# A graph network's first block: tile products ahead of the turns of the edge lists, the edge list sent later, 20 message fetches issued there

## What is computed

```python
h = jnp.maximum(_layernorm(x, axis=-1), 0.0)
hw = jnp.einsum('ni,rio->rno', h, weight)          # 8 relations and one for the node itself
msg = hw[rel, src] + bias[rel]
agg = jax.ops.segment_max(msg, dst, num_segments=n)
agg = jnp.where((in_deg > 0)[:, None], agg, 0.0)
x = x + jax.nn.relu(hw[-1] + agg + bias[-1])
```

## Time and profile before

| what | us |
|---|---|
| median of 3 runs | 2628.93 |
| lowest and highest run | 2625.03, 2635.14 |
| the profiled execution, whole | 2634.49 |
| its span in the profile | 2632.6 |

### The profile page before, as it was taken

How to read it: one execution, slowest core, us unless ns; L and a number is a source line. 1 busy time by engine, 2 the same in 40 slices (tenths; PEclk the granted TensorE clock), 3 DMA queues, 4 the chain that set the end, 5 groups by cost and what they waited for, 6 DMA issues and landing times. The chain is left out here.

```text
span 2632.6 us, 33489 instructions
## 1 busy us (share of the span) xinstructions
PE 1954.5 (74%) x11712; PEld 1074.2 (41%) x11712; DVE 1325.4 (50%) x3186; ACT 673.2 (26%) x1332; POOL 1470.4 (56%) x1528
## 2 busy tenths in 40 slices
PE   6844444545454545437899999998999999799996
PEld 2411111111111111115455555554555555467775
DVE  6466666666666666653322222321233332357775
ACT  3344454545454545433200000000000000100000
POOL 4277777777777777760256666664666666300000
PEclk8856665656556656568999999999999999899998
DMA  5545555555555555564444544565444444610000
GB/s 170 192 120 159 170 171 159 176 164 164 159 164 159 169 163 180 160 196 169 142 163 150 166 156 153 170 123 167 144 164 154 145 142 152 99 40 1 1 6 21
DMA packets 183330, 370.17 MB, mean 141 GB/s; under 512 B 38760, under 2 KB 119254, under 8 KB 174838
## 3 DMA queue, kind: packets, MB, share of 16 engines
q1 hardware_dynamic: 129208, 263.74, 28.3%
q0 software_dynamic: 48704, 101.21, 16.4%
q10 hardware_dynamic: 5246, 3.03, 0.4%
HBM read 232.54 MB, written 135.28 MB: 140 GB/s over the span
## 5 line engine op out<-in xcount | busy, mean ns | idle before, releaser
L925 POOL DMA_INDIRECT arena<-table_rel,key_rel x784 | 771.8, 984 | 277.9 <-issue 235.3
L1575 POOL DMA_INDIRECT arena<-table_cut,src_at x324 | 311.6, 962 | 275.3 <-DMA table_cut<-Z 111.9
L1040 PE MATMUL ps_t<-arena 128*128 128x50 f16 x1568 | 95.3, 212 | 471.8 <-DVE arena L953 471.8
L943 DVE SCALAR_TENSOR_TENSOR arena<-arena,keep_max 128x128 f32<-128x128 f32 x784 | 275.0, 351 | 332.4 <-DMA arena<-table_rel,key_rel 319.1
L1575 POOL DMA_INDIRECT arena<-table_next,src_at x324 | 313.3, 967 | 187.2 <-issue 91.7
L1097 ACT ACTIVATE arena<-ps_out 128x800 fp8e4<-128x800 f32 x512 | 399.8, 835 | 43.9 <-PE ps_out L1053 43.4
L1053 PE MATMUL ps_out<-arena 128*128 128x400 f16 x1024 | 370.9, 499 | 46.2 <-ACT arena L1097 46.2
L1853 PE MATMUL ps_out<-arena,Z 128*128 128x512 fp8e4 x1600 | 352.3, 380 | 0.0
L1853 PE MATMUL ps_out<-arena,cut 128*128 128x512 fp8e4 x1600 | 350.2, 379 | 0.0
L1040 PEld LDWEIGHTS ps_t<-arena 128*128 128x128 f16 x1568 | 78.2, 115 | 552.5 <-DVE arena L953 535.0
L959 DVE TENSOR_TENSOR arena<-iota,arena 128x1072 f16<-128x1072 f16 (+1 forms) x384 | 271.4, 707 | 0.0
(11 more groups left out here) (312 smaller groups left out, 1903.7 us busy)
## 6 DMA issues: line engine op xcount, KB each, us to landing
arena<-adjacency SPq DMA_DIRECT2D x64, 1600.0 KB, 7.1
adjacency<-arena SPq DMA_DIRECT2D x160, 320.0 KB
running_rows<-arena SPq DMA_DIRECT2D x392, 128.0 KB
arena<-adjacency_plain SPq DMA_DIRECT2D x50, 400.0 KB, 8.7
table_rel<-arena SPq DMA_DIRECT2D x25, 512.0 KB, 2.7
arena<-table_rel,key_rel POOLq DMA_INDIRECT x784, 2.9
adjacency_plain<-adj SPq DMA_DIRECT2D x50, 128.0 KB, 2.5
arena<-table_cut,src_at POOLq DMA_INDIRECT x324
```

The lines of the kernel that those rows point to most:

```text
L925: e.indirect_dma_start(message(t), None, table, bass.IndirectOffsetOnAxis(key[:, t:t + 1], 0)).then_inc(s_msg[t % both], 16)
L943: e.scalar_tensor_tensor(fold(t), fold(t - 1), g.keep_max[:, t:t + 1], message(t), ALU.add, ALU.max).then_inc(s_run, 1)
L1040: e.matmul(out[:, :, w * WIN:(w + 1) * WIN], g.hot_low[:, q % 2, w // 2, :, w % 2], g.hot_flat[:, q % 2, w // 2, :, w % 2].rearrange("p (a ...
L1575: e.indirect_dma_start(g.picked[:, w % 2 * BLOCKS + k, :, :].rearrange("p a f -> p (a f)"), None, tables[y], bass.IndirectOffsetOnAxis(g.s ...
```

## The change

In block 1:
- SP no longer sends the edge list ahead of all table stores, but between the stores of tiles 3 and 4 (`LISTED`).
- DVE leaves `variance` and `normal` of rounds 3 and 4 until the near destinations are counted; ACT takes `squares` of those rounds behind tiles 2 and 5 and `deviation` behind tiles 10 and 11. Tiles 0 and 1 come ahead of `squares(3)`.
- PE runs all 25 tiles and only then the 13 turns and three blocks. `turned` has two PSUM buffers (the second is where the tiles' transposes were, so that the first turn waits for the last of ACT's copies, `s_tT`); a turn waits for the reads of the last but one.
- POOL, behind its gathers of windows and blocks, waits for all table stores and issues the first 20 message fetches (`AHEAD`). What DVE keeps in the ring of messages at that time is moved into `g.Z`.

In block 2 POOL starts at fetch 20, and the wait of `step(t)` for `s_begun` counts from there.

```diff
+AHEAD, LISTED = 20, 4
-    spot0, valid = (msgf[:, 1408 + k * P:1408 + (k + 1) * P] for k in range(2))
+    spot0, valid = (g.Z[:, 8 + k, :] for k in range(2))
-    near_node, inside, code, real = (msgf[:, 1664 + k * P:1664 + k * P + RUN] for k in range(4))
+    near_node, inside, code, real = (g.Z[:, 10 + k, 0:RUN] for k in range(4))
-    turned = g.ps_t[:, 1, :].rearrange("p (f c) -> p f c", f=FIELDS)
+    turned = [g.ps_t[:, k, :].rearrange("p (f c) -> p f c", f=FIELDS) for k in range(2)]
@@ prepare, gpsimd, behind the gathers of L237
+            for k in range(2):
+                e.wait_ge(s_st[k], 16 * ((NT + 1 - k) // 2))
+            e.wait_ge(s_nst, 16)
+            for t in range(AHEAD):
+                e.indirect_dma_start(message(g, t), None, g.table8,
+                                     bass.IndirectOffsetOnAxis(g.key_rel[:, t:t + 1], 0)).then_inc(s_msg[t], 16)
@@ sync
-            e.wait_ge(s_list, 1)
-            e.dma_start(g.edge_list.rearrange(...), lists.rearrange(...)).then_inc(s_lst, 16)
             for n in range(NT):
+                if n == LISTED:
+                    e.wait_ge(s_list, 1)
+                    e.dma_start(g.edge_list.rearrange(...), lists.rearrange(...)).then_inc(s_lst, 16)
                 e.wait_ge(s_ev, n + 1)
@@ scalar
-            for r in range(2, TROUNDS):
-                squares(r)
-                deviation(r)
-                if r > 2:
-                    tile(r - 3)
-            for n in range(2, NT):
+            squares(2)
+            deviation(2)
+            for n in range(NT):
                 tile(n)
+                if n in (2, 5):
+                    squares(3 + n // 5)
+                if n in (10, 11):
+                    deviation(n - 7)
@@ vector
             normal(2)
-            variance(3)
             moments(4)
-            normal(3)
-            variance(4)
-            normal(4)
@@ behind s_ends (L437)
+            variance(3)
+            variance(4)
+            normal(3)
+            normal(4)
             e.wait_ge(s_begin, 1)
@@ tensor, turn
-                if gr:
-                    e.wait_ge(s_read, 2 * gr)
+                if gr == 0:
+                    e.wait_ge(s_tT, NT)
+                elif gr == 1:
+                    e.wait_ge(s_win, 4)
                 else:
-                    e.wait_ge(s_win, 4)
+                    e.wait_ge(s_read, 2 * gr - 2)
                 for f in range(FIELDS):
-                    last = e.transpose(turned[:, f, :], windows[gr][:, f::FIELDS], g.ident[:, :])
+                    last = e.transpose(turned[gr % 2][:, f, :], windows[gr][:, f::FIELDS], g.ident[:, :])
@@ tensor
-                if n >= NT - GROUPS + 1:
-                    turn(n - (NT - GROUPS + 1))
-            turn(GROUPS - 1)
+            for gr in range(GROUPS):
+                turn(gr)
@@ aggregate_and_build
-            for t in range(STEPS):
+            for t in range(AHEAD, STEPS):
-                e.wait_ge(s_begun, min(t + BEHIND, STEPS))
+                if t + BEHIND > AHEAD:
+                    e.wait_ge(s_begun, min(t + BEHIND, STEPS) - AHEAD)
```

More of the change, by code:

```diff
@@ L134, in edge_rows, with prepare @@
     yield tile[P - 1:P, 0:E - (P - 1) * STEPS], ap[(P - 1) * STEPS:E].rearrange("(a t) -> a t", a=1)
-def prepare(g, weight, bias):
+def prepare(g, weight, bias, s_msg):
     nc = g.nc
@@ L469, in _ @@
                 at = slice(gr * P, (gr + 1) * P)
+                fields = turned[gr % 2]
                 e.wait_ge(s_turn, gr + 1)
-                step(e.scalar_tensor_tensor(spot0, turned[:, 0, :], float(-gr * P * WIN), twice, ALU.add, ALU.subtract))
+                step(e.scalar_tensor_tensor(spot0, fields[:, 0, :], float(-gr * P * WIN), twice, ALU.add, ALU.subtract))
                 step(e.scalar_tensor_tensor(valid, spot0, -1.0, spot0, ALU.add, ALU.mult))
-                e.scalar_tensor_tensor(g.low[:, at], valid, 0.0, turned[:, 1, :], ALU.is_equal, ALU.mult).then_inc(s_read, 1)
-                e.scalar_tensor_tensor(g.both_spots[:, :, at], turned[:, 2:4, :], 2.0,
+                e.scalar_tensor_tensor(g.low[:, at], valid, 0.0, fields[:, 1, :], ALU.is_equal, ALU.mult).then_inc(s_read, 1)
+                e.scalar_tensor_tensor(g.both_spots[:, :, at], fields[:, 2:4, :], 2.0,
                                        spot0.unsqueeze(1).to_broadcast([P, 2, P]), ALU.mult, ALU.add).then_inc(s_read, 1)
@@ L479, in _ @@
                 e.wait_ge(s_turn, GROUPS + k + 1)
-                fields = [turned[:, f, 0:RUN] for f in range(FIELDS)]
+                fields = [turned[(GROUPS + k) % 2][:, f, 0:RUN] for f in range(FIELDS)]
                 step(e.scalar_tensor_tensor(near_node, fields[0], float(-(DENSE + k * (RUN // CAP // PARTS_OF)) * P), bases,
@@ L579, in _, with message @@
             e.matmul(g.ps_t[0:1, 0, 0:1], g.whole[:, :], g.ones[:, 0:1], start=True, stop=True).then_inc(s_order, 1)
+def message(g, t):
+    return g.msg[:, t % (2 * HALF) // HALF, t % HALF, :]
 class Norm:
@@ L860, in scalar, with aggregate_and_build @@
                          scale=g.inv_dev[:, n:n + 1]).then_inc(self.s_h, 1)
-def aggregate_and_build(g, table, key, params):
+def aggregate_and_build(g, table, key, params, s_msg):
     nc = g.nc
-    s_msg = [g.sem(f"msg{u}") for u in range(2 * HALF)]
     s_out = [g.sem(f"rout{h}") for h in range(2)]
@@ L889, in pairs_before @@
         return sum(b < FULL for b in order[:q]) * PAIRS
-    def message(t):
-        return g.msg[:, t % both // HALF, t % HALF, :]
     def fold(t):
@@ L924, in _ @@
                 e.sem_inc(s_begun, 1)
-                e.indirect_dma_start(message(t), None, table,
+                e.indirect_dma_start(message(g, t), None, table,
                                      bass.IndirectOffsetOnAxis(key[:, t:t + 1], 0)).then_inc(s_msg[t % both], 16)
@@ L942, in step @@
                     e.wait_ge(s_run, t)
-                e.scalar_tensor_tensor(fold(t), fold(t - 1), g.keep_max[:, t:t + 1], message(t),
+                e.scalar_tensor_tensor(fold(t), fold(t - 1), g.keep_max[:, t:t + 1], message(g, t),
                                        ALU.add, ALU.max).then_inc(s_run, 1)
@@ L2131, in gnn_kernel @@
         g.ps_out = ctx.enter_context(nc.psum_tensor("ps_out", [P, 2, 1536], F32))
-        prepare(g, a["L0_gnn_weight"].rearrange("r k o -> k r o"), a["L0_gnn_bias"].rearrange("r o -> (r o)"))
-        aggregate_and_build(g, g.table8, g.key_rel, plain_params(g, a))
+        s_msg = [g.sem(f"msg{u}") for u in range(2 * HALF)]
+        prepare(g, a["L0_gnn_weight"].rearrange("r k o -> k r o"), a["L0_gnn_bias"].rearrange("r o -> (r o)"), s_msg)
+        aggregate_and_build(g, g.table8, g.key_rel, plain_params(g, a), s_msg)
         g.recycle()
```

7 lines of the change are left out of this document (4 added, 3 removed).

## The result

| | before | after |
|---|---|---|
| median, us (20 runs each) | 2633.39 | 2619.32 |
| lowest and highest | 2625.03, 2637.59 | 2613.59, 2629.08 |
| the profiled execution: whole, span | 2634.49, 2632.6 | 2618.36, 2615.5 |

The changed kernel takes 0.995 of the time, with an interval of 0.994 to 0.9959: 14.1 us less, where 23.3 were forecast. The time forecast was 2606 us with a range of 2592 to 2619, and 2619.32 lies just above it. Both kernels ran 20 times; the 3 runs shown of before had a median 4.5 us lower than these 20.

What follows compares the result with a forecast made beforehand. Block 2 was taken to be bound by POOL's issue of 784 message fetches. Gain 29.3 less 6 us given back is 23.3; from the median 2628.9 that gives 2605.6, rounded 2606 us, range 2592 to 2619.

Steps and rivals of the forecast that it cites:

- T: Block 1: the end of the tile stage (last tile's bias), forecast at 98.4 us, 18.5 us before 116.86.
- The stall goes: Block 1, tiles 0 to 11: ACT's 13.34 us wait for the first store vanishes; tile 11 ends at 55.0, 15.1 us gained.
- The moved normalisation: Block 1, DVE: variance and normal of rounds 3 and 4 fit its idle time; cost nothing, or up to 1 us.
- Tiles 12 to 24: Block 1: tiles without turns take 2.78 us each, plus 2.5 us for gathers; stage ends at 98.4, 18.5 us gained.
- The rival of a late tile stage: Block 1: low clock or contention ends the stage near 108 to 112, 2617 us; with a larger stretch, chance 0.13.
- The turns behind: Block 1: 13 windows at 1.33 us and three blocks follow the tiles; DVE leaves at 126.5; move costs about 10 us.
- 20 fetches in block 1: Block 1, POOL: starts 4.8 us after the tile stage, fetches take 25.0 us, POOL leaves at 128.2, behind DVE.
- no charge: Block 1: fetches beside DVE's reads of windows are not stretched, citing 0.94 us at 74.58; priced at nothing.
- Block 2 starts 1.1 us later: Boundary of blocks 1 and 2: fetch 20 starts about 1.1 us after POOL's last, at 129.3 us; 29.3 us gained.
- What block 2 gives back: Start of block 2: DVE, catching up out of step, stretches about 24 fetches; 6 us lost, bounds 0 and 13.
- The last rival (the port to the end): Block 2: DVE stays out of step and stretches fetches to the end; 0.5% slower, about 2642 us; chance 0.04.

Runs made afterwards that it cites:

- experiment 4: Kernel before plus only the 20 fetches issued in block 1; old order of tiles and turns, edge list first, normalisation where it was: ratio 1.001 to before.
- experiment 8: Kernel before, with POOL's drain (its wait for the DMAs it issued) left out at the end of block 1: ratio 1.0009 to before.
- experiment 13: The changed kernel itself, run again on another chip: 2620.63 us, ratio 0.9957 to before.
- Experiment 6: Changed kernel, but the edge list is sent ahead of all table stores again (LISTED = 0): ratio 0.999 to before.
- Experiment 7: Changed kernel, but 12 turns stand between tiles 13 to 24 again, in one PSUM buffer: ratio 0.9954 to before.
- experiment 1: Changed kernel without POOL's drain (its wait for the DMAs it issued) at the end of block 1: 2612.97 us, ratio 0.9922 to before.
- experiment 2: Changed kernel with 12 fetches ahead instead of 20 (AHEAD = 12): 2625.37 us, ratio 0.9966 to before.
- experiment 5: Changed kernel, but the one-hots of block 2's first 60 folds read their indices from PSUM instead of SBUF: ratio 0.9954 to before.
- 14: Changed kernel without POOL's drain at the end of block 1, run again on another chip: 2612.47 us, ratio 0.9922 to before.
- 9: The changed kernel itself, run again on a chip where every kernel took some 2950 us: ratio 0.9969 to before.
- 15: Changed kernel without POOL's drain at the end of block 1 and with 28 fetches ahead: 2613.60 us, ratio 0.9929 to before.
- 3: Changed kernel with no fetch taken ahead (AHEAD = 0), only the new order of block 1: ratio 1.0006 to before.
- 16: Changed kernel without POOL's drain at block 1's end, turns between the tiles again, 8 fetches ahead: 2611.84 us, ratio 0.992 to before.

## Why the prediction was right and wrong

The difference, first between the two profiled executions: fetch 20 came 23.0 us earlier (158.56 and 135.56), fetch 20 to 60 took 5.4 us more (51.65 and 57.08), fetch 60 to 783 0.6 less. That makes 18.2 at fetch 783. Behind it 1.1 us went in the later layers, to which the change does nothing, and 1.0 outside the span, which gives 16.1 for the whole executions. The one of before lay 1.1 over its median of 20, the one of after 1.0 under its own: 14.1.

That pair of executions flatters the change. The old order of block 1 has two more profiles: T was 114.64 us in experiment 4 and 113.05 in experiment 8 (before without the drain), against 116.86. The new order has eight, with T from 97.0 to 103.3 and 99.8 in the mean. So T moved by some 15 us in the mean and not by 17.8 (an estimate from these eleven profiles). Fetch 783 of experiments 8 and 13, taken as second profiles of before and after, lies at 1138.2 and 1129.4; with two profiles of each the difference there is 13.5 us, close to the 14.1 of the medians.

1. *The stall goes*: right. Tile 11 ended at 55.58 us, forecast 55.0, with no wait of ACT over 1.5 us in tile 2. Experiment 6 shows it the other way round.
2. *The moved normalisation*: no cost that shows. `begins` starts at 55.51, right behind tile 11.
3. *Tiles 12 to 24*: right for the changed kernel, T = 99.07 for 98.4, but the 18.5 us gained were counted from an execution of before whose T was late (above). The rival of a late tile stage (T of 108 and more) didn't happen; experiment 6 shows what it looks like, 2628 us. Its price rested on a misreading: from 43.43 to 56.21 us three tiles passed, not two, with transposes at 48.72 and 53.42 between; the two slow ones took 5.3 and 4.7 us, the third 2.8.
4. *The turns behind*: right, DVE left at 126.87 for 126.5. That the move costs about 10 us by itself doesn't follow from the step's own figures: T + 28.1 against T + 15.5 is 12.6, and 12.3 was measured. Experiment 7 shows that this cost is covered whole and buys nothing.
5. *20 fetches in block 1*: first at 104.25 for 103.2, POOL through at 129.52 for 128.2. Of these 1.3 us 0.7 is T and 0.3 the fetches: the first ten, beside DVE's reads of windows, took 1.00 to 1.02 us instead of 0.94. That is this execution's and not a rule: in experiments 1, 2, 5, 6, 13 and 14 the fetches of block 1 took 0.94 us in the mean, beside the same reads. The row given for "no charge" (74.58) lies ahead of DVE's first read of a window (81.29) and shows nothing of it; the gathers behind that read in the same trace do, with 0.94 to 0.95 us but for one of 1.03.
6. *Block 2 starts 1.1 us later*: **this step failed.** It was 6.04 us, and fetch 20 started at 135.56 instead of 129.3. The price was taken from the one row of before, where fetch 0 follows DVE's last instruction by 1.24 us. In that row POOL had stood idle for 39.24 us, so that it could not show what the block's end costs an engine with 20 DMAs just issued. In its place the runs show a drain of 6.0 us on POOL: the gap is 0.3 us without it (experiments 1 and 14), and without it before is no faster (experiment 8). Step 5 had found that POOL would now be the last to leave; the step behind it priced the boundary as if it were DVE. The trace of before had no block end with POOL last, so this cost wanted bounds from both sides, as other unseen costs had, and got one value.
7. *What block 2 gives back*: the size was right, 5.4 us to fetch 60 and 4.8 to fetch 783 for 6, and so was its end after some 20 fetches. The mechanism, a fetch held by DVE's instruction, is supported by experiment 5 and the table of arrears; that one fetch can be held by several in a row the step did not have. The last rival (the port to the end) didn't happen: from fetch 60 on the mean fetch is as before, 983 and 984 ns.

The sum then reads 23.3 - 1.3 (step 5) - 4.9 (step 6) + 1.2 (step 7) = 18.3 at fetch 783, where the profiles show 18.2. The 4.2 us from there to the 14.1 of the medians are the spread of executions, of which the late T of the profiled execution of before is the part that can be named. The prediction saw that this execution lay 5.6 us over its median and took the gain over to the median unchanged. The forecast time has a second error that no step made: it started from a median of three, 2628.93, and 20 runs gave 2633.39. Of the 13.7 us between 2605.6 and 2619.32, 4.5 are the baseline's, and 9.2 the gain's.

## What to carry to other kernels

Work moved ahead of a barrier has to be through the barrier's wait: ask what the engine must wait for before it may leave, and take the price from a row where that engine was the last one, not from one where it stood idle. Two parts that are each worth nothing alone can be worth something together when one makes a chain the longer one and the other shortens that chain; run each alone before either is called useful. And a consumer's head start is not free where its catching up holds the producer: the five us here were paid once per head start and grew with it, and putting the catching up off (experiment 5) only moved the bill, which came out larger. Last, a gain counted from one profiled execution is as uncertain as that execution: take two of the kernel before, where the stage in question varies.

## What was unexpected of the hardware

**The end of a block behind indirect DMAs.** 6.0 us in seven profiles (after, 4, 5, 6, 7, 9 and 13), whenever it began, and 0.3 us without the drain where DVE was through first (1, 14 and 15). Where POOL had been through 8 us (experiment 2) or 39 us (before) ahead of the others, nothing of it was left on the path. Where the profiles show their landing (after, 4, 7 and 13), the fetches of block 1 landed 2.4 to 2.6 us behind their issue, so the landing of the last one doesn't fill the 6.0 us. What else the drain waits for isn't shown.

**POOL's queue runs through a barrier.** Without the drain, DVE began block 2 while POOL still had 9 fetches of block 1 to start (131.26 us, experiment 15).

**A fetch can be held for several instructions of DVE in a row**: 3.88 us for one whose bare time is 0.94, while DVE went without a pause through four folds and five one-hots of at most 0.71 us each (experiment 5).

**The tile stage ends anywhere between 97.0 and 103.3 us with the same order of tiles** (after and experiments 1, 2, 3, 5, 13, 14 and 15), and most of it is handed on: experiment 13, the changed kernel again, had T 4.2 us, fetch 20 3.4 and fetch 783 4.6 us later than the first profile. Of the 4.2 us 2.9 are there by tile 1 already, together with a lower clock of TensorE; the rest came between tiles 17 and 20. Stretch 14 to 25 us (us, then busy and count of PE, PEld, DVE, ACT, POOL, then the granted clock, the DMA share and GB/s) of the changed kernel and of its second profile, experiment 13:

```profile
14.00:25.00 11.00, 7.72 (x21) 3.55 (x21) 10.50 (x34) 6.24 (x27) 8.15 (x8) 0.69 0.25 67
```

```profile
14.00:25.00 11.00, 7.59 (x14) 3.35 (x15) 10.50 (x35) 6.28 (x27) 8.02 (x8) 0.50 0.24 59
```

With the clock at half (1.2 of 2.4 GHz) through that stretch PE got 14 of its groups of matmuls begun instead of 21, and tile 1's bias came some 2.4 us later in the three such profiles (3, 13 and 15: 26.95 to 27.39, against 24.00 to 25.55 in eight others: after, 1, 2, 5, 6, 7, 14 and 16). DVE, ACT and POOL were busy for nearly the same time in both. What made the clock rise in one execution and not in the other, with the same program, the profiles don't show. A difference of T of 6 us or less between two kernels, one profile each, therefore says nothing by itself.
